# One layer-0/Mamba kernel on one core: the Silu of the convolved inputs on four row groups instead of two

## What is computed

```python
xz = h @ W_in
xm, z = jnp.split(xz, 2, axis=-1)
xc = conv1d(transpose(xm), conv_w, 4 causal taps, one group per channel) + conv_b
xm = silu(transpose(xc))                       # the activation that the change is about
dtr, Bm, Cm = split(xm @ W_xp, [64, 80])
dt = softplus(dtr @ W_dt + b_dt)
def step(hst, inp):                            # over time, state (channels, 16)
    hst = hst * exp(dt_t[:, :, None] * A) + (dt_t * x_t)[:, :, None] * B_t[:, None, :]
    return hst, einsum('bds,bs->bd', hst, C_t)
y = (ys + xm * D_param) * silu(z)
out = x + gate * inverse_permuted(y @ W_out)
```

## Time and profile before

| | us |
|---|---|
| median of 3 runs | 3439.36 |
| lowest and highest | 3436.74, 3440.71 |
| span of the profiled execution (the page gives no other time for it) | 3433.5 |
| busy: TensorE | 2862.0 (83%) |
| busy: VectorE | 2457.5 (72%) |
| busy: GpSimd | 1818.2 (53%) |
| busy: ScalarE | 1597.8 (47%) |

### The profile page before, as it was taken

The page is one execution under the profiler, slowest core; times in us unless marked ns, Lnnn a source line. Parts: engine busy times, 40 slices in busy tenths (PEclk is TensorE's granted clock), DMA queues, the critical chain, the costliest instruction groups (busy, mean ns, idle before and its releaser), DMA issues.

```text
span 3433.5 us, 37791 instructions
## 1 busy us (share of the span) xinstructions
PE 2862.0 (83%) x11066; PEld 1598.6 (47%) x11066; DVE 2457.5 (72%) x3184; ACT 1597.8 (47%) x2252; POOL 1818.2 (53%) x771
## 2 busy tenths in 40 slices
PE   7999999999999987687877887887877877887774
PEld 3545454554545443345445445445445444444442
DVE  3444444444444244999999998999999999999992
ACT  1122122222212215576676675676675675676550
POOL 0121111112111112778689689689688689689791
PEclk9999999999999997787997987987987987988877
DMA  5002020110202222332353353354353353353362
GB/s 189 6 25 80 0 79 31 48 59 21 79 0 80 86 70 71 67 73 67 76 117 94 77 121 91 77 117 93 77 121 90 77 124 88 81 125 89 88 135 62
DMA packets 193931, 270.53 MB, mean 79 GB/s; under 512 B 16877, under 2 KB 82545, under 8 KB 193738
## 3 DMA queue, kind: packets, MB, share of 16 engines
q1 hardware_dynamic: 146152, 183.53, 16.7%
q0 software_dynamic: 44032, 83.91, 13.9%
q10 hardware_dynamic: 3554, 0.88, 0.1%
HBM read 167.32 MB, written 42.22 MB: 61 GB/s over the span
## 4 chain that ended last, share of the span: by engine, by line
DVE 26%; issue 15%; PE 7%; POOL 5%; ACT 4%; DMA 4%; DVEq 1%; POOLq 0%; SPq 0%; ACTq 0%
DVE hs L1640 13%; DVE acc L1681 8%; POOL hs L1517 3%; PE bank L1210 2%; DMA fin<-y_rows,idx_first 2%; DVE xm L1608 2%; PE bank L1153 1%; ACT bank L1395 1%; DVEq L110 1%; POOL acc L1536 1%; PE bank L1183 1%; DMA b_wide<-b_rows 1%; PE bank L1177 1%; DMA out<-fin 1%; PE bank L1236 1%
## 5 line engine op out<-in xcount | busy, mean ns | idle before, releaser
L1517 POOL TENSOR_TENSOR hs<-u,b_wide 128x2048 f32<-128x2048 f32 x256 | 1280.7, 5026 | 75.4 <-DVE u L1632 75.2
L1640 DVE TENSOR_TENSOR_SCAN hs<-bank,hs 128x512 f32<-128x512 f32 x1024 | 1229.5, 1213 | 29.1 <-POOL hs L1517 16.5
L1210 PE MATMUL bank<-ident,hs 128*128 128x128 f32 x4096 | 750.3, 319 | 358.2 <-DVE hs L1640 237.4
L1395 ACT ACTIVATE bank<-dt,decay 128x512 f32<-128x512 f32 x1024 | 697.9, 689 | 622.6 <-DVE hs L1640 621.0
L1210 PEld LDWEIGHTS bank<-ident,hs 128*128 128x128 f32 x4096 | 560.9, 163 | 892.3 <-issue 525.9
L1681 DVE SCALAR_TENSOR_TENSOR acc<-bank,c_t,acc 128x512 f32<-128x512 f32 x800 | 585.4, 732 | 91.1 <-PE bank L1210 80.9
L1153 PE MATMUL bank<-h_t,w_in 128*128 128x512 f32 x1024 | 547.6, 622 | 9.7 <-ACT h_t L1326 5.4
L1536 POOL DMA_DIRECT2D acc<-scaled x224 | 254.3, 1135 | 321.9 <-ACT scaled L1402 298.9
L1236 PE MATMUL bank<-w_y,zs 128*128 128x512 f32 x512 | 260.2, 599 | 3.5 <-DVE fin L1698 2.5
L726 POOL TENSOR_TENSOR y_rs<-y_var,mhalf 128x8 f32<-128x8 f32 x8 | 16.0, 2002 | 440.4 <-DVE y_var L200 440.4
L585 PE MATMUL bank<-z_t,w_k 128*128 128x512 f32 x512 | 221.8, 594 | 5.8 <-ACT z_t L682 5.8
(11 more groups left out here) (154 smaller groups left out, 3079.2 us busy)
## 6 DMA issues: line engine op xcount, KB each, us to landing
acc<-scaled POOLq DMA_DIRECT2D x224, 256.0 KB, 4.1
w_in<-in_L_cond_W_in SPq DMA_DIRECT2D x128, 256.0 KB, 4.0
b_wide<-b_rows SPq DMA_DIRECT2D x128, 256.0 KB, 3.7
z<-in_x SPq DMA_DIRECT2D x8, 2048.0 KB, 8.3
res<-in_x SPq DMA_DIRECT2D x8, 2048.0 KB, 8.3
x_rows<-res SPq DMA_DIRECT2D x7, 2048.0 KB, 7.4
fin<-x_rows SPq DMA_DIRECT2D x56, 256.0 KB, 2.8
out<-fin SPq DMA_DIRECT2D x56, 256.0 KB, 2.0
```

What stands on the lines that cost most here:

```text
L1210: last = nc.tensor.transpose(state_banks[n % len(state_banks)][:, j * P:(j + 1) * P], hs[:, q % RING, j, t * P:(t + 1) * P], ident[:, :])
L1395: nc.scalar.activation(decay_bank(k)[:, :], dt[:, par, j, :], ACT.Exp, scale=g.decay[:, j, s:s + 1]).then_inc(da_ready, 1)
L1517: nc.gpsimd.tensor_tensor(hs[:, q % RING, :, :], u[:, 4 * half:4 * half + 4, :], b_wide[:, s % 2, :].unsqueeze(1).to_broadcast([P, 4, CHUNK]),
L1640: nc.vector.tensor_tensor_scan(block, decay_bank(k)[:, :], block, 0.0, ALU.mult, ALU.add).then_inc(scanned, 1)
```

## The change

silu_x takes a half (four groups) instead of a pair. In a turn it is called at n = 41 and n = 57 instead of 33, 41, 49 and 57; in the front after the taps of four groups instead of two. It waits for the taps of the last two of its four groups. xm_ready counts two per batch instead of four, and the waits of project_xd, dt_x and finish_dt are written for that.

```diff
@@ -1160,7 +1160,7 @@
                     pe.wait_ge(weights_loaded, 2 * DMA)
                     claimed(pe, place, "xd", 0)
                 for j in js:
-                    need(pe, xm_ready, KI // 2 * it + j // 2 + 1)
+                    need(pe, xm_ready, 2 * it + j // 4 + 1)
                     last = nc.tensor.matmul(work_bank(place, "xd", 0)[0:XD, :], w_xp[:, j, :], xm[:, j, :], start=(j == 0), stop=(j == KI - 1))
                 if js[-1] == KI - 1:
                     last.then_inc(fills(place, "xd", 0), 1)
@@ -1332,10 +1332,10 @@
                 nc.scalar.activation(xm[:, m, :], src[:, :], ACT.Identity, scale=g.taps[:, m, TAPS - 1:TAPS],
                                      bias=column(g, "L1_cond_conv_b", m)).then_inc(first_tapped, 1)
 
-            def silu_x(place, pair):
-                for m in (2 * pair, 2 * pair + 1):
+            def silu_x(place, half):
+                for m in (4 * half + 2, 4 * half + 3):
                     need(act, *read_by(place, "xm", m))
-                part = xm[:, 2 * pair:2 * pair + 2, :]
+                part = xm[:, 4 * half:4 * half + 4, :]
                 nc.scalar.activation(part, part, ACT.Silu).then_inc(xm_ready, 1)
 
             def keep_z(place, m):
@@ -1423,8 +1423,8 @@
                             rows_normed_by_act(nc, g, b + 1, b + 1)
                         if 17 <= n < 17 + KD:
                             norm_modulated(b + 1, 1 - par, place, n - 17)
-                        if n in (33, 41, 49, 57):
-                            silu_x(place, (n - 33) // 8)
+                        if n in (41, 57):
+                            silu_x(place, n // 57)
                         if n == 65:
                             keep_xd(b + 1, place)
                         if n == 74:
@@ -1445,10 +1445,10 @@
             def front(it, par, place):
                 for i in range(KD):
                     norm_modulated(it, par, place, i)
-                for pair in range(KI // 2):
-                    first_tap(place, 2 * pair)
-                    first_tap(place, 2 * pair + 1)
-                    silu_x(place, pair)
+                for half in range(2):
+                    for m in range(4 * half, 4 * half + 4):
+                        first_tap(place, m)
+                    silu_x(place, half)
                 keep_xd(it, place)
                 keep_c(par, place)
                 for half in range(2):
@@ -1500,7 +1500,7 @@
 
             def dt_x(it, par, half):
                 need(pool, dt_ready, 2 * it + half + 1)
-                need(pool, xm_ready, KI // 2 * it + 2 * half + 2)
+                need(pool, xm_ready, 2 * it + half + 1)
 
                 need(pool, inputs_ready, HALVES * it - 2 + half + 1)
                 part = slice(4 * half, 4 * half + 4)
@@ -1628,7 +1628,7 @@
                 part = slice(4 * half, 4 * half + 4)
                 add_dt(it, par, half)
                 need(dve, dt_ready, 2 * it + half + 1)
-                need(dve, xm_ready, KI // 2 * it + 2 * half + 2)
+                need(dve, xm_ready, 2 * it + half + 1)
                 nc.vector.tensor_tensor(u[:, part, :], dt[:, par, part, :], xm[:, part, :], ALU.mult).then_inc(u_ready, 1)
 
             def scan(it, k):
```

## The result

The changed kernel takes 3451.76 us (median of 7 runs, 3447.17 to 3456.94) against 3439.36 us (7 runs, 3436.74 to 3442.8): ratio 1.0038, 95% interval 1.0028 to 1.0049. It is slower by 12.4 us, and the interval is clear of 1. The forecast was +7.7 us and a range of 3438 to 3457: direction and range hold, the size is short by 4.7 us.

The account below looks back on a forecast made before the run. VectorE was taken to bound the turns, with ScalarE's total hardly mattering. 5.99 us at n = 57 plus 1.70 in the front made +7.7 us, 3441.2 span, 3447.0 us with 5.9 us for the median; range 3438 to 3457.

Parts of the forecast that it names:

- ScalarE's saved work is worth 0: In the turns, 38.8 us of Silus and table loads removed gain 0, hidden by ScalarE's idle time before scans.
- n = 41 costs nothing: The Silu at n = 41 grows by 0.855 us, within 2.0 us of slack before VectorE's addition: cost 0.
- n = 57: Longer Silu delays scaled copy, transposes and VectorE's addition: wait 1.55 us in place of 0.70, seven times, +5.99 us.
- The front, +1.7: Once, before the turns: eight projection matmuls wait for the last Silu, ScalarE's copy at 1323.4 instead of 1321.72, +1.7 us.
- Rival A: TensorE's clock falls in the longer gap at n = 57: about 1.2 us a turn, 8.4 in all, 3455; chance 0.18.
- A clock of 0.50 there: Sign of being wrong: TensorE's granted clock at the n = 57 addition reads 0.50 (1.2 GHz).
- Everything behind is paced by VectorE's scans and moves with it: Behind n = 57, the 0.855 us a turn only shifts later work, leaving the term at 7 x 0.855 = +5.99 us.
- The range: 3438 to 3457 us for the whole kernel, taking in Rival B's break-even and Rival A.
- The forecast's own spread: About 3 us to either side of the forecast time, as the three runs differ by 4 us and dips move.
- Rival B: From n = 70 to 110, shifted low-clock dips give back up to 2.3 us a turn, 16 in all (3431); chance 0.20.
- C: ScalarE's saved time in the turns counts in full: 38.8 us go, giving 3400.6; chance 0.04.

Follow-up runs that it names:

- e5: Changed kernel with both four-group Silus of a turn moved behind the scaled copy (n = 42, 58) and the front's Silus in pairs: 3430.02 us, ratio 0.9982.
- e10: Kernel before with the first half in one Silu at n = 42, pairs at n = 50 and 58, a count for each pair: 3427.26 us, ratio 0.9975.
- e6: Kernel before with only the last two-group Silu moved from n = 57 to 58, behind the scaled copy: 3425.41 us, ratio 0.9971.
- e4: Changed kernel with the second half's Silu split into pairs at n = 49 and 57, coarse count kept: 3438.42 us, ratio 1.0002.
- e3: Changed kernel with the second Silu of a turn moved from n = 57 to 58, behind the scaled copy: 3432.65 us, ratio 0.9987.
- e9: Kernel before plus one ScalarE copy of 912 columns behind the Silu of n = 57: 3453.22 us, ratio 1.0050.
- e2: Kernel before with the changed front alone (two Silus of four groups there): 3438.63 us, ratio 1.0003.
- e11: Changed kernel with six products by zeros on TensorE ahead of the late transposes of n = 57: 3447.90 us, ratio 1.0037.
- e1: Changed kernel with pairs again in the front, so the turns' part of the change alone: 3452.66 us, ratio 1.0043.
- e8: e5 with the first Silu of z also moved behind a scaled copy, from n = 92 to 94: 3429.62 us, ratio 0.9982.
- e12: e6 with two unused 512-column statistics more on VectorE at n = 20 of the turns that prepare a batch: 3442.22 us, ratio 1.0016.
- e7: The changed kernel unaltered, run once more for a second profile: 3450.03 us, ratio 1.0041.

## Why the prediction was right or wrong

- *ScalarE's saved work is worth 0*: right, and stronger than said. ScalarE waits 38.4 us more for scans, and neither e5 nor e10 is faster than e6, where the work is all there.
- *n = 41 costs nothing*: right. No wait of VectorE stands there after either, and e4, which keeps that Silu, is level with before.
- *n = 57*: the mechanism is right to the number, 1.55 us forecast, 1.55 or 1.56 measured in four turns, TensorE's gap 2.1 forecast, 2.04 to 2.11 measured. e3, e4 and e9 show it from both sides.
- *The front, +1.7*: 1.6 in the profile, and this close by luck, since two errors cancel. The last Silu started at 1318.18, not 1317.90, and ScalarE's copy of the projection came at 1323.85, where 1323.4 was worked out (1321.72 before), 2.1 us late; then 0.5 us came back behind it, where TensorE's clock fell later against its matmuls of dt than before. By itself e2 measures 1.0 us with an interval that holds 0.
- *Rival A* was dismissed too far: not instead of the forecast but on top of it. In three turns of seven the clock did fall at the gap, 0.7 to 1.0 us each, about 2.5 us in sum; e11 shows that it is TensorE's pause. A clock of 0.50 there was one of the prediction's own signs of being wrong, and it showed in these three turns.
- *The step that was wrong* is "Everything behind is paced by VectorE's scans and moves with it". The falls of the clock behind n = 57 don't move with the scans: early in 4 turns before, in 6 after. The term of +5.99 us measured two to three times that: 12.5 us between the first scan and the last in the two profiles, +15.0 in the turns alone (e1), and e9 +17.3 for 7 x 0.83 = 5.8 us. In the other direction e6 gives -10.5 us for the 4.9 us of wait taken away; e3, e5 and e8, which take the same wait away but keep the coarse count, give -5.0 to -6.3, little more than its length (e3 with the longer front in it).
- *The range* holds because it was widened for rival A. The forecast's own spread, 3 us to either side of 3447.0, doesn't reach 3451.76.
- *Rival B* named the right place (S lies in the first part of its stretch) and the wrong sign. The prediction took the differences between turns as luck without direction; they have one. S is 16.7 to 23.3 us in the five kernels without the wait and with nothing added (1 to 4 early falls), 23.0 to 25.3 with the short wait (three kernels, 3 or 4), 28.2 to 33.8 with the long one (the changed kernel twice and three others, 6 or 7).
- *C* is refuted by the result itself, and by e5 and e10 against e6.

What stays open is why a longer turn makes more falls of the clock come early: the profiles show that they do, not why. e5's and e10's difference stays open too, and what e8 asked. It is not open that a faster kernel than both exists: e6, the kernel before with 57 made 58, takes 3425.41 us, ratio 0.9971.

## What to carry to other kernels

Where an engine isn't the bound, its total is worth nothing, but the length of one piece in its queue can be: look at what short, urgent instruction stands behind the long one, and move the long one behind it before making it larger. A delay in a turn can cost a multiple of itself where the clock of another engine rises and falls within the turn, so measure the exchange rate with a known delay (e9, e12) rather than count it once. Before a piece is moved behind an urgent one, look also at what comes next in the queue: it may be urgent too (e8).

## What the runs showed of the hardware that was not expected

- A microsecond of delay on VectorE cost 1.7 to 3 in this kernel where nothing else was changed with it: 4.9 us of waits removed gave 10.5 us (e6), 5.8 us added gave 17.3 (e9), at most 9.5 us of work added gave 15.7 (e12 against e6). With the coarse count kept, 4.9 us removed gave 5.0 to 6.3 (e3, e5, e8).
- A gap of 2.0 to 2.1 us of TensorE at n = 57 was followed by a fall of its clock in 12 turns of 28 (after 3, e7 2, e1 4, e9 3), a gap of 1.18 to 1.25 us in none of 21 (before, e2, e4), and with 1.47 us of products put ahead of the transposes in none of 7 (e11).
- TensorE's clock falls in every turn behind n = 57, at one of two times some 8 us apart, and the early one costs VectorE about 2 us more of waits there. Longer turns had more of the early ones: 1 to 4 of 7 in the kernels without the long wait, 5 in e12, 6 or 7 with it.
- A load of ScalarE's table took 1.283 us, and the next instruction began 0.01 to 0.02 us after its end, at all 28 loads before a Silu on xm in the turns of the kernel before and at all 14 of the changed one.
